# Attention block with fp32r matmuls: the weight of masked keys moved out of P into a term of its own

## What is computed

```python
qkv = x @ w_qkv.T + b_qkv
scores = jnp.einsum('bhfc,bhtc->bhft', k, q)
scores = jnp.where(causal, scores, -10000.0)      # key f is seen by query t where f <= t
attn = jax.nn.softmax(scores, axis=-2)            # over the keys f
vals = jnp.einsum('bhft,bhfc->bhtc', attn, v)
out = vals @ w_o.T + b_o
```

## Time and profile before

| | |
|---|---|
| median of 3 runs | 1454.84 us (1454.34 to 1454.89) |
| span of the profiled execution (its own time, from first to last instruction) | 1453.0 us |
| what lies around the span, against the median | 1.8 us |
| busy share of the span | TensorE 99%, its weight loads 88%, VectorE 63%, ScalarE 48%, GpSimd 43% |
| attention phase, output phase | about 858 us, about 595 us |
| one batch of the loop | 102 us |

### The profile page before, as it was taken

One profiled execution on the slowest core, in us unless ns is written; L12 is line 12 of the kernel. 1 busy time (PEld: TensorE's weight loads), 2 busy tenths in 40 slices (PEclk: granted clock), 3 DMA queues, 4 the chain that ended last, 5 costly groups with the idle time before them and its releaser, 6 DMA issues.

```text
span 1453.0 us, 24689 instructions
## 1 busy us (share of the span) xinstructions
PE 1436.8 (99%) x7852; PEld 1280.6 (88%) x7852; DVE 920.2 (63%) x2118; ACT 692.4 (48%) x1497; POOL 623.7 (43%) x1154
## 2 busy tenths in 40 slices
PE   7999999999999999999999999999999999999998
PEld 6888888888888888888888889999999999999998
DVE  7576575675675775765855887655555555555554
ACT  6365465564574673654654763333333323333332
POOL 3353451461553452533622584444443344444442
PEclk9999999999999999999999999999999999999999
DMA  7212113113122122121122722322222222222211
GB/s 251 83 41 70 58 35 101 32 26 101 36 54 69 40 54 79 40 58 65 40 58 91 207 88 102 102 102 102 100 82 85 101 101 87 101 101 101 94 69 62
DMA packets 51540, 118.72 MB, mean 82 GB/s; under 512 B 5552, under 2 KB 22192, under 8 KB 51504
## 3 DMA queue, kind: packets, MB, share of 16 engines
q1 hardware_dynamic: 51504, 118.27, 25.7%
HBM read 60.06 MB, written 25.69 MB: 59 GB/s over the span
## 4 chain that ended last, share of the span: by engine, by line
PE 95%; DMA 1%; POOL 1%; DVE 1%; ACT 1%; issue 0%; POOLq 0%; DVEq 0%
PE ps_f L2036 26%; PE ps_o L1391 20%; PE ps_o L1422 12%; PE ps_o L1987 11%; PE ps_s L1443 5%; PE ps_t L1301 4%; PE ps_v L1275 4%; PE ps_o L1385 3%; PE ps_v L1276 2%; PE ps_f L2017 2%; PE ps_o L1345 1%; PE ps_x L2006 1%; PE ps_t L1391 1%; PE ps_t L1284 1%; DMA valsT<-vt 1%; POOL wagl L616 1%
## 5 line engine op out<-in xcount | busy, mean ns | idle before, releaser
L2036 PE MATMUL ps_f<-wagh,x2Th 128*128 128x364 f32 x768 | 255.1, 332 | 0.4 <-POOL wagl L616 0.4
L2036 PE MATMUL ps_f<-wagh,x2Tl 128*128 128x364 f32 x768 | 252.6, 329 | 0.0
L2036 PE MATMUL ps_f<-wagl,x2Th 128*128 128x364 f32 x768 | 252.5, 329 | 0.0
L1391 PE MATMUL ps_o<-xTh,wh 128*128 128x512 f32 x424 | 174.1, 411 | 0.0
L1391 PE MATMUL ps_o<-xTh,wl 128*128 128x512 f32 x424 | 166.8, 393 | 0.0
L1391 PE MATMUL ps_o<-xTl,wh 128*128 128x512 f32 x424 | 165.9, 391 | 0.0
L2036 PEld LDWEIGHTS ps_f<-wagh,x2Th 128*128 128x128 f32 x768 | 144.3, 188 | 2.0 <-POOL wagl L616 0.7
L2036 PEld LDWEIGHTS ps_f<-wagl,x2Th 128*128 128x128 f32 x768 | 144.7, 188 | 1.1
L2036 PEld LDWEIGHTS ps_f<-wagh,x2Tl 128*128 128x128 f32 x768 | 144.5, 188 | 0.0
L558 POOL TENSOR_TENSOR cw<-wm,cnt 128x4 f32<-128x4 f32 x64 | 12.9, 202 | 299.8 <-ACT pr L1061 299.8
L731 DVE TENSOR_TENSOR PT<-ps_t,PT 128x512 fp32r<-128x512 f32 (+1 forms) x192 | 109.6, 599 | 41.2 <-ACT PT L1026 39.2
(11 more groups left out here) (222 smaller groups left out, 3494.6 us busy)
## 6 DMA issues: line engine op xcount, KB each, us to landing
kst<-kst SPq DMA_DIRECT2D x64, 256.0 KB, 3.7
xt<-in_x SPq DMA_DIRECT2D x32, 512.0 KB, 4.0
x2r<-x2n SPq DMA_DIRECT2D x30, 512.0 KB, 2.9
xs<-in_x SPq DMA_DIRECT2D x24, 512.0 KB, 4.4
out<-x SPq DMA_DIRECT2D x23, 512.0 KB, 3.0
valsT<-vt SPq DMA_DIRECT2D x64, 128.0 KB, 2.3
vraw<-valsT SPq DMA_DIRECT2D x32, 256.0 KB, 3.4
raw<-in_wqkvT SPq DMA_DIRECT2D x12, 512.0 KB, 5.9
```

The lines of the kernel that those rows point to most:

```text
L1391: done = pe.matmul(ps[:, :], w[:, k, c:c + P], xT[:, k, :], start=(k == 0 and w is wh and xT is xTh), stop=(k == KD - 1 and w is wl), skip ...
L2036: last = pe.matmul(ps_f[:, g, 0:GW], a[:, k, :], w[:, k, cols], start=(k == 0 and a is xh and w is wagh), stop=False, skip_group_check=True)
```

## The change

The weights of all 512 keys are split another way: vals = sum over visible keys of (P - wn) v + wn times the total of v over all 512 keys.

- `normalise` computes (exp - wm) / sum in one two-operation instruction each, with `nwm` = -wm, which `denominator` now writes as one more small instruction; a `pool.drain()` stands before the four.
- `diagonal` writes to one of two places (`DIAGONALS`), and waits for the values of two heads before (`pv_done`, which starts at 2) in place of the copy.
- `masked_weights` and `masked_spread` go, with `wt_ready` and `wn_done`.
- `values` reads high and low rows at the visible columns alone, and adds one matmul: `totals` of the head (its high and low part side by side, 128 columns) by the diagonal, 384 columns. It waits for `d_ready` just ahead of it, and in head 0 for `totals_low`.
- Once per batch the total of v is made: ScalarE copies tile 0 to `vsum`, VectorE adds tiles 1 to 3 (an instruction ahead of each of those tiles' low parts), ScalarE and VectorE split the sum (`vsum_hi`, `vsum_lo`, at the end of slot 1, ahead of the third group of P of head 0), TensorE multiplies it by ones (`value_totals`, two matmuls of 512 columns, in slot 2 where `masked_weights` of head 0 stood), and `totals_hi`, `totals_lo` split the result; `totals_lo` stands after `scores_max` of slot 2.
- `dynamic_dma_scratch_size=1024` is given to the program.

```diff
             def denominator(h, b):
...
                 pool.tensor_tensor(den[:, q, :], cw[:, q, :], acc[:, q, :], ALU.add).then_inc(den_ready, 1)
+                pool.tensor_tensor(nwm[:, q, :], wm[:, q, :], mone[:, :].to_broadcast([P, 4]), ALU.mult)
...
             def diagonal(h, b):
-                pool.wait_ge(wn_done, H + 1)
-                pool.wait_ge(wt_ready, 1 + H)
-                pool.tensor_tensor(W_DIAGONAL.rearrange("p (i t) -> p i t", i=3),
+                pool.wait_ge(pv_done, H + 1)
+                pool.tensor_tensor(DIAGONALS[q].rearrange("p (i t) -> p i t", i=3),
...
             def normalise(h, b):
+                pool.drain()
                 for i in range(NT):
-                    last = pool.tensor_scalar(at, at, rden[:, q, i:i + 1], 1.0, ALU.mult, ALU.mult)
+                    last = pool.tensor_scalar(at, at, nwm[:, q, i:i + 1], rden[:, q, i:i + 1], ALU.add, ALU.mult)
...
             def v_lo(t, b):
                 dve.wait_ge(v_high, 4 * b + t + 1)
+                if t > 0:
+                    dve.wait_ge(v_low, 4 * b + t)
+                    done = dve.tensor_tensor(vsum[:, :], ps_j[t % 2][:, :], vsum[:, :], ALU.add)
+                    if t == NT - 1:
+                        done.then_inc(vsum_ready, 1)
...
+            def vsum_lo(b):
+                dve.wait_ge(vsum_high, b + 1)
+                dve.tensor_tensor(vsum_l[:, :], vsum[:, :], vsum_h[:, :].bitcast(F32), ALU.subtract).then_inc(vsum_low, 1)
+            def totals_lo(b):
+                dve.wait_ge(totals_high, b + 1)
+                dve.tensor_tensor(totals[:, :, HD:2 * HD], ...,
+                                  totals[:, :, 0:HD].bitcast(F32), ALU.subtract).then_inc(totals_low, 1)
...
-            def masked_spread(h, b):
-                act.wait_ge(t_full[1], 2 * (8 * b + h) + 2)
-                act.activation(W_SPREAD, ps_t[1][:, 0:3 * P].rearrange("p (n c) -> p n c", n=3), ACT.Copy)\
-                    .then_inc(wt_ready, 1)
+            def vsum_hi(b):
+                act.wait_ge(vsum_ready, b + 1)
+                act.activation(vsum_h[:, :], vsum[:, :], ACT.Copy).then_inc(vsum_high, 1)
+            def totals_hi(b):
+                act.wait_ge(totals_full, b + 1)
+                act.activation(totals[:, :, 0:HD], ps_t[1][:, :].rearrange("p (h c) -> p h c", h=NH), ACT.Copy)\
+                    .then_inc(totals_high, 1)
...
         def values(pe, h, b):
-            pe.wait_ge(wt_ready, 1 + H + 1)
...
             for j in range(NT):
-                pe.matmul(ps_v[:, :], v[:, j, h, :], HIGH_ROWS[j], start=(j == 0), stop=False, skip_group_check=True)
-                last = pe.matmul(ps_v[:, j * P:], v[:, j, h, :], LOW_ROWS[j], start=False, stop=(j == NT - 1),
-                                 skip_group_check=True)
+                for rows in (HIGH_ROWS[j], LOW_ROWS[j]):
+                    pe.matmul(ps_v[:, j * P:], v[:, j, h, :], rows, start=(j == 0 and rows is HIGH_ROWS[0]), stop=False,
+                              skip_group_check=True)
+            pe.wait_ge(d_ready, H + 1)
+            if h == 0:
+                pe.wait_ge(totals_low, b + 1)
+            pe.matmul(ps_v[:, 0:3 * P], totals[:, h, :], DIAGONALS[h % 2], start=False, stop=True,
+                      skip_group_check=True).then_inc(pv_done, 1)
-        def masked_weights(pe, h, b):
-            pe.wait_ge(d_ready, H + 1)
-            pe.wait_ge(t_lo, 3 * H + 2)
-            pe.matmul(ps_t[1][:, 0:3 * P], ones[:, 0:1].to_broadcast([P, P]), W_DIAGONAL,
-                      start=True, stop=True).then_inc(t_full[1], 1)
+        def value_totals(pe, b):
+            pe.wait_ge(vsum_low, b + 1)
+            pe.wait_ge(t_lo, 3 * 8 * b + 2)
+            for part in (vsum_h, vsum_l):
+                last = pe.matmul(ps_t[1][:, :], ones[:, 0:1].to_broadcast([P, P]), part[:, :],
+                                 start=(part is vsum_h), stop=(part is vsum_l))
+            last.then_inc(totals_full, 1)
```

More of the change, by code:

```diff
@@ L235, in attention_phase @@
         PT = sb("PT", [P, ROOM * P], F32R)
+        totals = sb("totals", [P, NH, 2 * HD], F32R)
+        vsum = sb("vsum", [P, PART], F32)
+        vsum_h = sb("vsum_h", [P, PART], F32R)
+        vsum_l = sb("vsum_l", [P, PART], F32R)
         ones = sb("ones", [P, 2], F32R)
@@ L300, in attention_phase @@
         v_low = sem("v_low")
+        vsum_ready = sem("vsum_ready")
+        vsum_high = sem("vsum_high")
+        vsum_low = sem("vsum_low")
+        totals_full = sem("totals_full")
+        totals_high = sem("totals_high")
+        totals_low = sem("totals_low")
         k_dup = [sem(f"k_dup{i}") for i in range(2)]
@@ L846, in body @@
                         scores_max(h, b)
+                    if h == 2:
+                        totals_lo(b)
                     if 1 <= h <= 3:
@@ L896, in last_body @@
                 v_lo(3, b)
+                vsum_lo(b)
                 p_lo(0, 2, b)
                 scores_max(2, b)
+                totals_lo(b)
                 vals_sum(0, b)
@@ L1484, in steps @@
                 items = between(BETWEEN_LAST if last else BETWEEN, h, part, b)
-                if part == 0 and h >= 2 and len(items) == 1:
+                if part == 0 and h == 2:
                     kind, p, row, ks = items[0]
@@ L1489, in steps @@
                     step(kind, p, row, ks, last)
-                    if n == 0 and part == 0 and h >= 2:
-                        masked_weights(pe, h - 2, b)
+                    if n == 0 and part == 0 and h == 2:
+                        value_totals(pe, b)
             def turns(h, place, b):
@@ L1519, in last_body @@
             def last_body(b):
-                whole, first, second = range(W.KV), range(W.KV // 2), range(W.KV // 2, W.KV)
+                whole = range(W.KV)
                 scores(0, b)
@@ L1525, in last_body @@
                     else:
-                        tile_product(h - 5, 1, first)
-                        masked_weights(pe, h - 2, b)
-                        tile_product(h - 5, 1, second)
+                        tile_product(h - 5, 1, whole)
                     if h >= 2:
@@ L1541, in last_body @@
                         transpose_p(pe, h - 1, 2, b)
-                tile_product(3, 1, whole[:1])
-                masked_weights(pe, NH - 2, b)
-                tile_product(3, 1, whole[1:2])
+                tile_product(3, 1, whole[:2])
                 values(pe, NH - 2, b)
@@ L2040, in ffn @@
                             last_transposes(pe)
-                        if first and g == 2 and k == 2:
-                            last_weights(pe)
                         if first and g == 2 and k == KD // 2:
@@ L2118, in _ @@
             attention.tensor(pe)
-            output.tensor(pe, attention.last_transposes, attention.last_weights, attention.last_values)
+            output.tensor(pe, attention.last_transposes, attention.last_values)
 def kernel(L0_attn_x, L0_attn_w_qkv, L0_attn_b_qkv, L0_attn_w_o, L0_attn_b_o, L0_ffn_W, L0_ffn_b, L0_ffn_A,
```

71 lines of the change are left out of this document (29 added, 42 removed).

## The result

The changed kernel takes 1457.4 us (median of 15 runs, 1456.6 to 1459.5) against 1454.6 us for the kernel before in runs on the same chips (15 runs, 1453.6 to 1455.1). The ratio is 1.0021, interval 1.0013 to 1.0028: slower by about 3 us, where 10 us less were forecast. The profiled executions have spans of 1457.3 and 1453.0 us; that of the changed kernel took 1459.1 us, 1.7 above its median, so what is counted from the two profiles comes out 1.5 us larger than between the medians.

What follows compares the result with a forecast made beforehand. TensorE was taken to bound the loop. Its 16.8 us saved, less 3.5 (slot 2), 1.0 (GpSimd waits), 1.6 and 0.8 (last batch), gave 9.9 us off: 1444.9 us, range 1439.5 to 1451.5.

Steps and rivals of the forecast that it cites:

- TensorE is the bound: Attention loop: TensorE bounds it, so time taken from it counts in full until another engine is late; net 2.1 us per batch.
- I take 0.08 for one of the two: P times v, per head: of two 128-column matmuls one costs 0.06 us, the other 0.08; group with diagonal 1.355 us.
- The end of the range that I kept for it: Short matmuls, low end: 0.12 us more per head than taken, so 9 us net over 8 batches in place of 16.8.
- so no price there: GpSimd's four normalising instructions: the second per-partition operand costs nothing, so they still take 2.06 us.
- My rival on this: Slower normalising: 1.25 us more for the four, paid in slots 5 and 7; 1466 us, chance 0.10 with its milder form.
- A margin of 0.13 us: Slot 5: GpSimd's last normalising instruction ends at 216.03, TensorE's transposes start at 216.16, read as 0.13 us to spare.
- `split_x` gains 1.0: GpSimd, slot 5: `diagonal` no longer waits for ScalarE, so `split_x` starts at 203.0 in place of 204.0.
- Slot 2, 0.5 of wait: Slot 2: the new chain of the totals makes TensorE wait 0.5 us per batch, 3.5 us in 7 batches.
- These, and the new chain in slot 2, decide: Margins behind GpSimd's normalising of slots 5 (0.13 us) and 7 (0.75 us), with slot 2's chain, decide how much gain stays.
- The last batch: From slot 5 on a GpSimd, store and load chain: about 0.5 of 2.1 us kept, 1.6 lost, 0.8 added.
- The milder form of the slower rival: Waits of 2 us in slot 2 because VectorE's order slips: 1455 to 1458 us; chance 0.10 with the slower normalising.
- The signs of being wrong that the prediction named: A batch over 102 us, a normalising (L581) mean over 600 ns, or starts of short matmuls 0.11 us apart.

Runs made afterwards that it cites:

- spaced: The changed kernel with the eight matmuls of P times v reordered so that no two of 128 columns stand together: 1458.1 us, ratio 1.0023.
- before_two_operands: The kernel before with `nwm`, the drain and the two-operand normalising added and nothing else: 1459.4 us, ratio 1.0034.
- before_split_after: The kernel before with the last piece of `split_x` in slot 5 moved behind the normalising of head 5: 1454.0 us, ratio 0.9999.
- visible_only: The kernel before with high rows of P times v read at visible columns only, masked weights made but left out of the product: 1445.2 us, ratio 0.9939.
- no_drain: The changed kernel with semaphores in place of the drain ahead of the normalising: 1458.1 us, ratio 1.002.
- combined: The changed kernel with totals matmuls later, `split_x` piece behind the normalising, 128-column matmuls apart, semaphores for the drain: 1457.3 us, ratio 1.0018.
- late_totals: The changed kernel with the loop's two totals matmuls in slot 2 moved behind the six projection matmuls they stood amid: 1457.3 us, ratio 1.0021.

## Why the prediction was wrong, step by step

- **TensorE is the bound**: right, and TensorE did become shorter, by 1.35 us per batch against 2.1 forecast. The step that was too high is "I take 0.08 for one of the two": both short matmuls pay, and 1.44 us stand in place of 1.355, 5 us over 64 heads. `spaced` shows that another order of the same matmuls does not change it. The rule that I had discounted (the Trainium skill, "TensorE: Matmul & The Clock Gate", LDWEIGHTS: a load takes its columns over 1.2 GHz, 107 ns for 128) is borne out in the sum, where I tested it on single starts: with 0.107 for each of the two the nine would take 1.43 (an estimate from that page), and 1.44 was measured. The next start comes at 0.06, as I said, and the start after it at 0.11 (the earlier trace rows has one such pair only, with transposes behind it, and the scores group of the earlier trace rows showed the debt). The end of the range that I kept for it, 9 us net in place of 16.8, was nearer: 10.8 (8 x 1.35).
- **GpSimd's normalising**: "so no price there" is the step that failed, and the largest. I divided 1192 ns by 1024 elements and compared rates, and a cost per instruction can't be seen that way: the medians before rise by 0.83 ns per element from a start of 0.27 us, so 1024 elements with one operand would take 1.12 us and with 0.08 more 1.20 (an estimate from those medians), close to the 1.19 of `layernorm`. On 128 to 512 elements it is 0.33 us for the four. `before_two_operands` prices the whole part at 5 us. My rival on this had the mechanism right for slot 5 (no margin, so it pays) with an addition that was four times too large; the place of slot 7 had 0.62.
- **"A margin of 0.13 us"**: wrong, it was none, as `before_split_after` shows. With the margin at zero every saving of TensorE's ahead of it is lost as well, 0.45 of two heads (`visible_only` shows such a loss without any of the additions), and what I had as 0.1 of margin left in slot 6 became a wait of 0.8.
- **`split_x` gains 1.0**: the waiting of `diagonal` did go, but only some 0.3 came out. The piece's second wait was for ScalarE's copy (0.52 in the row at 213.05), which stands behind q's high part, and that behind TensorE's second half of q (0.53 at 206.34). That chain was already there, just behind the first: in the kernel before the copy ended at 211.95 and the piece started at 212.09.
- **Slot 2, 0.5 of wait**: right as a mechanism and nearly in size. Measured 0.43 (0.25 for `vsum_l`, the rest at the totals and the diagonal); 3.5 us forecast for the loop, 3 found. Not foreseen: the collision with the diagonal, which turned `no_drain` and `combined` into misses.
- **The other margins** were never worked out. "These, and the new chain in slot 2, decide" left out slot 3 (0.4) and underrated slots 7 and 8 (0.4). For slot 3 the last to end was q's low part, at the same distance as before, and `visible_only` shows that a saving of TensorE's is lost there; that q's low part is the cause was not tested by itself. Neither was the wait for `vals_sum`.
- **The last batch**: forecast 0.5 gained and 0.8 lost. Both kernels take 99.0 us from its first scores to the first feed-forward product, but kernels with the very same last batch took 98.0 (`late_totals`) and 99.0, so this stretch is not known to better than 1 us, and what the last batch gained or lost stays open.
- **The sum**: of 16.8 us, 6 were never there, and the waits of the loop took 14 (7 x 2.0) where 4.5 were expected. The milder form of the slower rival gave 1455 to 1458, which came out by luck: it had 2 us of wait in slot 2 from VectorE's order, and only 0.4 of the 2.0 stand there. The signs of being wrong that the prediction named all came: a batch over 102, a mean of the normalising instructions over 600 ns (634), and a start of 0.11 behind a short matmul.

## What to carry to other kernels

When the bounding engine gets shorter, the gain is worth only what the other engines' margins leave, so list every place where it waits on a semaphore, and before calling a distance a margin, find the distance at a place where it truly waits: equal distances mean zero margin. Price an added operand or a split matmul on the smallest instruction of its kind, since costs per instruction vanish in large ones. Before moving an instruction, ask who needs the buffer that it empties, not only who reads its result, and look for work that nobody waits for ahead of the late one: one such move turned this change from 3 us slower to 3 us faster.

## What the runs showed of the hardware that I had not expected

- A second per-partition operand adds 0.08 us to a GpSimd instruction of 128 to 512 elements per partition, whichever the size, and 0.33 to four together; a drain ahead of them costs 0.18.
- From GpSimd's end to TensorE's start lie 0.13 to 0.14 us, and the same from VectorE's `vsum_l` to the totals; from the end of q's low part to the load of the scores' first weights 0.33 to 0.34.
- VectorE's instruction on two tiles in SBUF and GpSimd's diagonal do not run side by side: the second to start is 0.45 us longer, so that 0.2 us less of GpSimd's work made TensorE 0.45 us later in slot 2.
- A 128-column matmul of this group lets the next one start after 0.06 us, and the start behind that one comes 0.05 late.
